# Attention scores and probabilities times v as full float32 products, one instruction per head, in a one-core decoder layer

## What is computed

```python
q = rmsnorm(q, q_norm_w); k = rmsnorm(k, k_norm_w)      # per head of 128
q = apply_rope(q, cos, sin); k = apply_rope(k, cos, sin)  # the position is the head's number here
scores = jnp.einsum('bhtd,bhsd->bhts', q, k) * scale
scores = LOGIT_SOFTCAP * jnp.tanh(scores / LOGIT_SOFTCAP)
scores = jnp.where(mask[None, None], -jnp.inf, scores)
attn = jax.nn.softmax(scores, axis=-1)
out = jnp.einsum('bhts,bhsd->bhtd', attn, v)
return out @ wo.T
```

## Time and profile before

| | us |
|---|---|
| median of three runs | 2131.62 |
| span of the profiled execution (first to last instruction) | 2047.4 |
| PE matmul busy | 1982.2 |
| PE weight load busy | 1790.4 |
| DVE busy | 1112.9 |
| POOL busy | 1013.5 |
| ACT busy | 917.8 |

### The profile page before, as it was taken

One profiled execution on the slowest core, in us unless ns is written; L12 is line 12 of the kernel. 1 busy time (PEld: TensorE's weight loads), 2 busy tenths in 40 slices (PEclk: granted clock), 3 DMA queues, 4 the chain that ended last, 5 costly groups with the idle time before them and its releaser, 6 DMA issues.

```text
span 2047.4 us, 40563 instructions
## 1 busy us (share of the span) xinstructions
PE 1982.2 (97%) x12012; PEld 1790.4 (87%) x12013; DVE 1112.9 (54%) x2413; ACT 917.8 (45%) x2119; POOL 1013.5 (50%) x1076
## 2 busy tenths in 40 slices
PE   6999999999999999999989999999999999999998
PEld 5788888888888888888878898899999999999997
DVE  4776666666677776777667555333333333333332
ACT  4555555554566666656555312233333333323332
POOL 5444444442344444544556206676733333588885
PEclk8999999999999999999989999999999999999999
DMA  8677777778877878788534238666633443499899
GB/s 321 199 240 257 254 255 253 256 254 279 295 256 282 322 252 304 279 280 288 199 117 167 93 104 284 210 217 216 229 122 121 123 129 123 143 214 218 193 213 242
DMA packets 188986, 450.47 MB, mean 220 GB/s; under 512 B 21696, under 2 KB 21952, under 8 KB 188864
## 3 DMA queue, kind: packets, MB, share of 16 engines
q1 hardware_dynamic: 135392, 338.68, 49.1%
q0 software_dynamic: 21504, 51.13, 10.6%
q10 hardware_dynamic: 31968, 59.12, 9.0%
HBM read 275.36 MB, written 173.48 MB: 219 GB/s over the span
## 4 chain that ended last, share of the span: by engine, by line
PE 84%; DVE 4%; DMA 3%; ACT 3%; POOL 2%; issue 2%; SPq 1%; ACTq 0%; POOLq 0%; DVEq 0%
PE bank L1139 21%; PE bank L979 15%; PE bank L1149 12%; PE bank L1030 7%; PE bank L1004 7%; PE bank L165 6%; PE bank L582 4%; PE bank L1016 3%; PE bank L592 3%; PE bank L599 2%; PE bank L1051 2%; PE bank L1063 1%; DMA xT<-xT_att 1%; DMA raw<-in_weights 1%; PE bank L1041 1%
## 5 line engine op out<-in xcount | busy, mean ns | idle before, releaser
L1139 PE MATMUL bank<-w_hi,xT 128*128 x1776 | 473.7, 329 | 2.3 <-DVE xT L1734 2.1
L979 PE MATMUL bank<-w_hi,xT 128*128 128x512 f32 x1024 | 356.3, 409 | 6.2 <-issue 3.3
L609 DVE TENSOR_TENSOR hT<-bank,hT 128x384 fp32r<-128x384 f32 x143 | 79.7, 557 | 472.5 <-ACT hT L606 472.5
L1139 PEld LDWEIGHTS bank<-w_hi,xT 128*128 128x128 f32 x1776 | 315.7, 188 | 10.3 <-issue 5.1
L1422 POOL TENSOR_TENSOR rr<-rr,expo 128x4 f32<-128x4 f32 x128 | 129.0, 1008 | 365.8 <-DVE rr L1620 365.8
L1139 PE MATMUL bank<-w_lo,xT 128*128 x888 | 286.3, 322 | 0.0
L979 PEld LDWEIGHTS bank<-w_hi,xT 128*128 128x128 f32 x1024 | 196.5, 192 | 47.3 <-issue 6.6
L1149 PE MATMUL bank<-w_hi,hT 128*128 x666 | 230.3, 400 | 2.4 <-DVE hT L609 2.4
L606 ACT ACTIVATE hT<-bank 128x384 fp32r<-128x384 f32 x143 | 70.2, 491 | 330.5 <-PE bank L599 319.5
L1004 PE MATMUL bank<-w_hi,xT 128*128 128x256 f32 x1024 | 214.1, 292 | 0.0
L979 PE MATMUL bank<-w_lo,xT 128*128 128x512 f32 x512 | 203.5, 398 | 0.0
(11 more groups left out here) (248 smaller groups left out, 4467.2 us busy)
## 6 DMA issues: line engine op xcount, KB each, us to landing
xT<-xT_att SPq DMA_DIRECT2D x126, 512.0 KB, 5.2
w_hi<-w_split SPq DMA_DIRECT2D x64, 512.0 KB, 6.7
w_lo<-w_split SPq DMA_DIRECT2D x64, 512.0 KB, 7.7
xg<-blank SPq DMA_DIRECT2D x111, 264.0 KB, 4.8
yg<-blank SPq DMA_DIRECT2D x111, 256.0 KB, 5.8
raw<-in_weights SPq DMA_DIRECT2D x82, 272.0 KB, 3.1
w_split<-w_hi SPq DMA_DIRECT2D x64, 272.0 KB, 3.4
w_split<-w_lo SPq DMA_DIRECT2D x64, 272.0 KB, 3.7
```

Source lines behind the costliest of these rows:

```text
L609: dve.tensor_tensor(hT[:, 1, :], src[:, 0:IP], hT[:, 0, :].bitcast(F32), ALU.subtract).then_inc(hT_lo, 1)
L979: last = pe.matmul(bank[par][:, :], xT[:, par, a, c * P:(c + 1) * P], w_hl[w][:, fw, c * 512:(c + 1) * 512], start=n == 0, stop=n == 11)
L1139: last = pe.matmul(out_[:, 0:I], xT[:, par, a, c * P:(c + 1) * P], flat(w_hl[w])[:, bass.ds(at + (c * 2 * I + half_ * I), I)], start=n == ...
```

## The change

`qkT`, `vE` and `pT` become plain float32 tiles without the second (low) copy. `pT` becomes two buffers by step parity instead of high and low. The scores are one instruction of 128 columns per head in every step, the probabilities times v one of 130 columns per head. L1615, L1623, L1652 and L1668 on DVE and L1271 on ACT are gone; POOL writes the masked probabilities straight to `pT` and waits for the product two steps back to have read that buffer (`pv_done`). ACT takes the tanh from PSUM in all steps, and PE waits for the last step's tanh before it writes `S_` again. The split of x, of the weights and of the normalised output `oT` stays.

```diff
-        qkT = sb_early("qkT", [P, 2, 512], F32R)
-        vE = sb_early("vE", [P, 4, 2, HG, 130], F32R)
-        pT = sb_early("pT", [P, 2, HG, T], F32R)
+        qkT = sb_early("qkT", [P, 512])
+        vE = sb_early("vE", [P, 4, HG, 130])
+        pT = sb_early("pT", [P, 2, HG, T])
...
                     if back:
 
-                        pe.wait_ge(p_hi, s - 1)
-                        pe.wait_ge(p_lo, s - 1)
-                        pe.wait_ge(v_hi, s - 1)
-                        pe.wait_ge(v_lo, s - 1)
+                        pe.wait_ge(p_done, s - 1)
+                        pe.wait_ge(v_out, s - 1)
                         for h in range(HG):
-                            for n, (a, w) in enumerate(TERMS):
-                                last = pe.matmul(O_[:, h * 130:(h + 1) * 130], pT[:, a, h, :],
-                                                 vE[:, (at4 - 2) % 4, w, h, :], start=n == 0, stop=n == 2)
+                            last = pe.matmul(O_[:, h * 130:(h + 1) * 130], pT[:, 1 - par, h, :],
+                                             vE[:, (at4 - 2) % 4, h, :], start=True, stop=True)
                         last.then_inc(pv_done, 1)
...
                     if mid:
-                        pe.wait_ge(qkT_hi, s)
-                        pe.wait_ge(qkT_lo, s)
-                        if wide(s):
...
-                        else:
...
+                        pe.wait_ge(qkT_out, s)
+                        wait(pe, th_done, 2 * s - 2)
+                        for h in range(HG):
+                            last = pe.matmul(S_[:, h * T:(h + 1) * T], qkT[:, (HG + h) * T:(HG + h + 1) * T],
+                                             qkT[:, h * T:(h + 1) * T], start=True, stop=True)
                         last.then_inc(s_done, 1)
...
-                        act.wait_ge(s_sum if wide(s) else s_done, s)
+                        act.wait_ge(s_done, s)
...
-                    if mid:
-                        act.wait_ge(mask_done, s)
-
-                        act.activation(pT[:, 0, :, :], heads(ex), ACT.Copy).then_inc(p_hi, 1)
...
                         pool.wait_ge(ex_done, s)
-                        pool.tensor_tensor(heads(ex), heads(ex), mask[:, :, :], ALU.mult).then_inc(mask_done, 1)
+                        wait(pool, pv_done, s - 2)
+                        pool.tensor_tensor(pT[:, par, :, :], heads(ex), mask[:, :, :], ALU.mult).then_inc(p_done, 1)
...
-                    if mid:
-                        dve.wait_ge(qkT_hi, s)
-                        dve.tensor_tensor(qkT[:, 1, :], QT_[:, :], qkT[:, 0, :].bitcast(F32),
-                                          ALU.subtract).then_inc(qkT_lo, 1)
...
-                        dve.wait_ge(v_hi, s + 1)
-                        dve.tensor_tensor(vE[:, at4, 1, :, 0:DH], heads(V_[:, 0:256]),
-                                          vE[:, at4, 0, :, 0:DH].bitcast(F32), ALU.subtract).then_inc(v_lo, 1)
...
-                    if mid and wide(s):
-                        dve.wait_ge(s_done, s)
-                        wait(dve, ex_done, s - 1)
-                        dve.reduce_sum(heads(th), S_[:, :].rearrange("p (h a n) -> p h n a", h=HG, a=2), AX.X)\
-                            .then_inc(s_sum, 1)
...
-                    if mid:
-                        dve.wait_ge(p_hi, s)
-                        dve.tensor_tensor(pT[:, 1, :, :], heads(ex), pT[:, 0, :, :].bitcast(F32),
-                                          ALU.subtract).then_inc(p_lo, 1)
```

More of the change, by code:

```diff
@@ L565, in wants @@
             return front, mid, back, tail, rec
-        def wide(s):
-            return not isinstance(s, int) or 1 <= s < SPLIT - 1
         def behind(s, fw, b, n):
@@ L1243, in step @@
                         wait(act, pv_done, s - 3)
-                        act.activation(vE[:, at4, 0, :, 0:DH], heads(V_[:, 0:256]), ACT.Copy).then_inc(v_hi, 1)
+                        act.activation(vE[:, at4, :, 0:DH], heads(V_[:, 0:256]), ACT.Copy).then_inc(v_out, 1)
                     if row_tile(s - 1) is not None:
@@ L1255, in step @@
                     if mid:
[L1256 removed]
+                        act.wait_ge(s_done, s)
                         act.wait_ge(rms_done, s)
[L1258 removed]
                         for h in range(HG):
[L1260 removed]
+                            act.activation(th[:, h * T:(h + 1) * T], S_[:, h * T:(h + 1) * T], ACT.Tanh,
                                            scale=rk[:, 1 - par, h:h + 1]).then_inc(th_done, 1)
                         act.wait_ge(th_done, 2 * s)
[L1263 removed]
+                        wait(act, p_done, s - 1)
                         act.activation(ex, th, ACT.Exp, scale=CAP).then_inc(ex_done, 1)
```

45 lines of the change are left out of this document (12 added, 33 removed).

## The result

The changed kernel takes **2068.22 us** (median of 4 runs, 2060.76 to 2077.50), the kernel before 2132.35 (4 runs): a ratio of 0.969, 95% interval 0.965 to 0.974. That is 64 us less, where the prediction said 43.

A forecast was written before the change was run, and what follows sets the result against it. PE was taken to bound attention. 40 us from PE's stream + 2.8 + 3 + 3 from stalls - 2.6 - 3 = 43 us, so 2131.6 - 43 = 2088.6 us; range 2070 to 2110.

The forecast's parts named there:

- The 84.2 us outside of the span: Whole run: 84.2 us were said to lie outside the profiled span of 2047.4 us and to stay fixed.
- group starts: At a group's first step PE waits for POOL's split piece; without L1615 0.4 us is won at seven steps, 2.8 us.
- the scores' 3: Second half, about twelve steps: scores and output transposes no longer wait behind L1615 and L1623 on DVE, 3 us won.
- the 3 us for GpSimd's late masks: First 100 us and end of attention: behind POOL's late mask ACT's copy and DVE's low part go, 3 us counted.
- The price of a full float32 product: Attention's scores and products with v: four passes for two heads, 0.44 us, against 0.61, 0.62 or 0.42 before.
- The rival on the other side: A full product takes four passes with a load each, 0.82 us for two heads, ending at 2190 us; chance 0.05.
- The trails: Delay behind narrow matmuls goes: 0.05 us behind products with v, 0.02 behind narrow scores, 7.7 us together.
- Neither bounds attention, so this is worth nothing by itself: Work leaving DVE and ACT in attention counts only where a chain through them makes PE wait.
- PE's stream: PE's matmuls in attention: cheaper products with v and narrow scores, and shorter delays behind them, 40 us together.
- -2.6 for the last seven steps: Attention's last seven steps: POOL and transfers set the pace, so PE's 0.4 us saved in each is lost.
- -3 for new waits for `xT`: Second half: in fifteen steps `xT` lands with small margins, so faster steps make PE wait, 3 us lost.
- The transfers (rival, 2116): Second half: transfers grow as fast as steps shrink, so 27 us of gain fall away, 2116 us; chance 0.09.

The follow-up runs named there:

- all side work kept: Changed kernel with VectorE's three low parts and sum and ScalarE's copy put back as dead work with their waits: 2106.18 us, 0.988 of the kernel before.
- scores' side work kept: Changed kernel with only the low part of q and k and the sum of the score halves put back as dead work with their waits: 2010.34 us.
- side work of the products with v kept: Changed kernel with only the low part of v, ScalarE's copy and the probabilities' low part put back as dead work with their waits: 2011.67 us.
- products with v alone: Kernel before with only the probabilities times v made full float32 products, the scores staying split: 2100.89 us, 0.985 of the kernel before.
- scores alone: Kernel before with only the scores made full float32 products (no L1615, no sum of halves), products with v staying split: 2097.62 us, 0.983.
- pairs: Changed kernel with scatters of rounds 2 to 5 issued two at a time between GpSimd's weight loads: 1996.93, 1999.43 and, on chip 10, 2007.27 us (0.941).
- the kernel before again: Kernel before, unchanged, run and profiled once more: 2134.4 us, ratio 1.000, span 2137.7 us.

## Why the prediction was right, and where it was wrong

**The 84.2 us outside of the span: this step failed.** It was taken "as fixed" and as outside. What the runs showed: it was the difference between an execution without stands and runs with them, and it shrank with the change. The numbers at hand could have warned: the profiled span lay 84 us under the median, while the runs agreed with each other within 16. The stands gave 9 to 14 of the 64 us: 64.1 measured, 49.7 and 54.9 in the two sets without them. Without this part the result would have been 2077 to 2083, by this estimate. The two profiled executions with stands agree in size, 88.1 us in the kernel before and 69.5 in the changed one. Most of the difference lies ahead of block 0, where the unchanged kernel stood 21.7 us and the changed one 2.7. The kernels with one half of the change stood 20.3 and 17.3 us there, the one with both halves and all side work kept 5.4. That this is the change's doing was not shown: it is one execution each, and the changed kernel's four runs lie in two groups, near 2062 and 2076, of which only the lower was profiled.

**Without the stands the forecast was near.** The sum said 2047.4 - 43 = 2004 for the span. It was 1996.8 and 1993.4, a gain of 51 and 54 us instead of 43. By stretch, the prediction's terms against the changed kernel in three executions (start of the step in the kernel before: 124.9, 511.7, 1020.5):

| stretch | predicted | measured |
|---|---|---|
| steps 0 to 12 | 3.9 | 6.8 to 9.9 |
| 12 to 64 | 13.2 | 13.7 to 13.8 |
| 64 to 120 | 24.1 | 20.5 to 24.0 |
| 120 to 127 | 1.9 | 6.1 to 7.8 |

(The first column deals out the prediction's terms: 0.20 us a step in the first half and 0.43 in the second, 2.8 for group starts in 12 to 64, the scores' 3 and the new waits' -3 in 64 to 120, and the 3 us for GpSimd's late masks half to the first and half to the last line, which also has the -2.6. The start in the kernel before is that of one execution; step 12 starts at 122.7 to 124.9 in five, median 124.6, and at 115.0 to 119.3 in the changed kernel's ten, median 117.)

The two middle lines are right. The 6 to 10 us that attention gained over the predicted 43 lie in the first and the last, which the prediction sized at 5.8 us together and which brought 15 to 16.

**The price of a full float32 product: right.** 0.44 and 0.45 us for four passes against 0.44. The rival on the other side, four loaded passes (0.82 us), has fallen: each instruction shows two loads and two matmuls. The Trainium skill, "FP8 and Floating Point Precision", section "TensorE Precision Notes", counts four passes for true FP32. The time agrees: one product of 128 columns takes 0.22 us, and a split v product of 256 columns 0.12 (703.39 - 703.27), so about 0.06 for 128. The records show two matmuls, not four. (The "four passes" of the prediction are those two matmuls for each of two heads.)

**The trails: right.** The steady step of the first half became 7.13 us (predicted 7.11), that of the second 7.13 (7.12). The first output product ends 703.59 + 0.47 - 703.84 = 0.22 us behind the products with v, 0.06 less than in the earlier trace rows.

**Group starts: right.** PE's excess there fell from 0.77 to 0.35 us (7.48 - 7.13) at five of them, to 0.71 at one. (The prediction reads 0.74 to 0.83 at seven; in the steps' lengths it is 0.77 to 0.86 at six and 1.6 at the seventh, step 63, which fell to nothing.) The rows that answer to the earlier trace rows, POOL's piece and PE's load behind it:

```profile
315.64 1.35 POOL L176 TENSOR_TENSOR w_lo<-raw,w_hi 128x544 fp32r<-128x544 f32 x1
...
317.06 0.19 PEld L975 LDWEIGHTS bank<-w_hi,xT 128*128 128x128 f32 x1 [0.31 <-issue]
```

With the scores' side work kept it is 0.39 more, the predicted 0.4; with that of the products with v kept it is 7.47 as in the changed kernel. That of the scores' two instructions it is L1615, which stands in the chain of the earlier trace rows, and not the sum, is argued from that place and was not tested apart.

**"Neither bounds attention, so this is worth nothing by itself": this step failed.** The prediction gave PE's stream 40 us and the side work 8.8. With the side work in place the faster stream is worth 17 us to step 127 (one execution), and the side work's removal after it 38. In the other order, side work away and the old passes kept, nothing was measured, so the 38 is its worth beside the faster stream only. That the total came out near is in part luck: both were done together, and what the one term has too much the other has too little. The reason is the one that the prediction named for single places only: work that is hidden beside a PE step of 7.31 or 7.54 us is not all hidden beside one of 7.13. The longer steps with the side work kept show that; it should have been asked of every wait, at the new step length.

**-2.6 for the last seven steps: not paid.** They gained 6 to 8 us, where the prediction's terms gave 1.9. POOL's mask now writes what PE reads, so there the chain was shorter by a whole copy and subtraction; with the side work of the products with v kept, these steps take 60.7 us instead of 56.4 to 58.5.

**-3 for new waits for `xT`: right, and paid.** PE's waits for `xT` in the second half are 3.3 us in the profile of the result, inside the predicted 2 to 6, but that is the lowest of ten executions of the changed kernel: they reach 7.6, with 5.5 in the middle, against 0.3 to 3.3 (1.0 in the middle) in five of the kernel before. So some 4 us are new. The transfers (rival, 2116) gave no more than that back: their share rose from 0.78 to 0.82.

**The first 12 steps: missed.** 6.8 to 9.9 us are gained there instead of 3.9 (7.6 between the medians). The steps 4, 6, 8 and 10 took 9.71, 9.71, 9.72 and 8.71 us and take 7.77, 7.78, 7.78 and 7.63 now: 6.9 us. Most of it hangs on the scores' side work: with it kept the first three take 9.3 and step 12 starts at 123.6, and in the kernel with the change for the products with v alone they take 9.4 and step 12 starts at 123.3. Without it they take 8.0 (scores alone) and 7.9 (side work of the products with v kept). PE's transposes wait there until VectorE has made the low part (`stage`) of a row transposed before. From 55 to 110 us, in the kernel before and in the one with the scores' side work kept, where L165 is L167 (the changed kernel has no such wait):

```profile
PE bank L165 <- DVE stage L1535: 2.1, 3, 0.7
```

```profile
PE bank L167 <- DVE stage L1510: 4.4, 3, 1.5
```

The prediction put its 1.5 us here on GpSimd's late masks, and missed that VectorE was late with this low part. Which part of the side work makes it late, the low part of q and k or the sum, was not separated.

## What to carry to other kernels

When the engine that sets the pace gets faster, price every hidden chain again at the new step length: here the faster passes with the side work kept brought 17 us of 55 in attention, and the other 38 came only when the side work, which the faster form makes unnecessary, went too. Where a profile's span and the runs' median lie apart by much more than the runs scatter, they are not the same kind of execution; find what differs before taking the rest as fixed. And a long row of indirect DMAs from GpSimd is better broken up between its other work, in a kernel like this one: it cost nothing on the chips without stands, and where the kernel before took 2137 us the changed one with pairs took 2007, against its 2068 in another set, with before at 2132.

## What the hardware showed that was not expected

**Scatter rounds that stop the other engines, on some chips.** In four profiled executions on chip 11 and in that of the result, rounds of 16 indirect DMAs in a row, 1.27 us apart, come with stands that delay a block by 14 to 18 us. At the blocks 10, 16 and 23 PE runs dry behind the seventh scatter, ScalarE behind the fourth to sixth. PE goes on 1 to 4 us behind the end of the last one, and in one case (the kernel before again, block 10) already between the fifteenth and sixteenth: so that the whole round has landed is not what ends a stand. Where it begins, ScalarE's next instruction is released (1320.53) and doesn't start (1336.55). ScalarE had just issued a transfer of its own, and it reads two table entries into registers ahead of that instruction (`value_load`), so either could be what is held. Ahead of block 0 it does neither, and an instruction is held there too. In the kernel before again, with a round of scatters from 1231.6 to 1252.3, PE's and ScalarE's lines:

```profile
1247.34 0.61 PE L599 MATMUL bank<-ident,hid 128*128 128x128 f32 x3 [2.44 <-DVE hid L616]
...
1254.73 0.49 ACT L606 ACTIVATE hT<-bank 128x384 fp32r<-128x384 f32 x1 [16.03 <-remote]
```

L606 is released at 1247.95 and starts 6.8 us later; one step earlier (L599 ends at 1237.82) it starts after 0.04 us. The transfers that bring instructions don't explain it: in the changed kernel's trace none runs between 1252 and 1440.5 us, and PE runs dry at 1265, 1323, 1381 and 1445 us. Chips 14 and 15 showed no stand in any profiled execution with the same rounds of 20 us. What holds the released instruction, and what makes the sets differ (the chip or the time), stays open.

**The clock after a stand.** PE's granted clock falls after it has stood. Busy time in the changed kernel behind the stand shown above, two stretches:

```profile
1337.00:1342.00 5.00, 4.12 (x10) 3.26 (x11) 2.26 (x4) 1.19 (x4) 0.00 (x0) 0.51 0.21 54
```

```profile
1342.00:1352.00 10.00, 10.00 (x64) 9.47 (x63) 2.26 (x4) 3.19 (x7) 0.00 (x0) 1.00 0.24 79
```

PE had been idle for 15.01 us; the clock is at 0.51 (the 1.2 GHz level) in the first stretch, in which it works again, and at 1.00 (2.4 GHz) in the next. So a stand costs a little more than PE waits: 15.01 us of waiting and 17.0 us of delay here.
